# The last layer's gate weights move beside its first products, and its last products go tile by tile to the output

## The reference

```python
x = _rmsnorm(src + sa, norm1_w)              # rows of 256, 512 of them
shared = _swiglu(flat @ W_shared_in) @ W_shared_out
g_probs = jax.nn.softmax(flat @ Wg_gate + group_bias, -1)      # 2 groups
g_idx = jnp.argmax(g_probs, axis=-1)
e_logits = flat @ We_gate + expert_bias                        # 8 experts
e_probs = jax.nn.softmax(jnp.where(in_group, e_logits, -jnp.inf), -1)
p_expert = e_probs * g_prob
topv, topi = jax.lax.top_k(p_expert, TOPK)                     # w: top 2, else 0
h = _swiglu(flat @ W1_shared)                                  # silu(a) * b
for e in range(E):
    routed = routed + h @ W2_experts[e] * w[:, e:e + 1]
out = _rmsnorm(x + (shared + routed), norm2_w)                 # added to the layer's input
```

## Time and profile before

| what | value |
|---|---|
| median of 3 runs | 2666.93 us (2666.87 to 2674.51) |
| the profiled execution's own time | 2669.26 us |
| its span, first to last instruction | 2667.4 us |
| TensorE busy | 2354.3 us, 88% of the span |
| DVE busy | 1460.5 us, 55% |
| ACT busy | 1055.5 us, 40% |
| mean granted TensorE clock | 0.921 of full speed |

### The profile page before, as it was taken

The page is one execution under the profiler, slowest core; times in us unless marked ns, Lnnn a source line. Parts: engine busy times, 40 slices in busy tenths (PEclk is TensorE's granted clock), DMA queues, the critical chain, the costliest instruction groups (busy, mean ns, idle before and its releaser), DMA issues. The chain is left out here.

```text
span 2667.4 us, 38992 instructions
## 1 busy us (share of the span) xinstructions
PE 2354.3 (88%) x15232; PEld 1367.6 (51%) x15232; DVE 1460.5 (55%) x2285; ACT 1055.5 (40%) x1896; POOL 381.9 (14%) x659
## 2 busy tenths in 40 slices
PE   2899999988999998999997687886879999988778
PEld 1344444435699663454453444352238657464547
DVE  4777877623222456888884685226976332323333
ACT  2466666612111233777774372124422233120310
POOL 2454000000000400000001250002630000000000
PEclk8799999998999997999999768987999999888789
DMA  7977553120554699456430001001025240101100
GB/s 197 234 186 166 103 114 57 26 99 2 228 204 175 167 302 236 93 93 133 93 60 35 12 1 61 29 1 65 0 91 178 95 174 0 52 1 51 54 0 8
DMA packets 108359, 258.62 MB, mean 97 GB/s; under 512 B 11824, under 2 KB 83088, under 8 KB 94224
## 3 DMA queue, kind: packets, MB, share of 16 engines
q1 hardware_dynamic: 104144, 213.73, 30.1%
q0 software_dynamic: 2736, 39.37, 4.4%
q10 hardware_dynamic: 1296, 3.03, 0.3%
HBM read 211.26 MB, written 44.83 MB: 96 GB/s over the span
## 5 line engine op out<-in xcount | busy, mean ns | idle before, releaser
L704 DVE TENSOR_REDUCE sta_parts<-sta_psA 128x1 f32<-128x1024 f32 x544 | 626.0, 1188 | 187.4 <-PE sta_psA L621 185.7
L762 ACT ACTIVATE sta_probs<-sta_psS 128x512 f32<-128x512 f32 x1056 | 575.8, 596 | 274.1 <-PE sta_psS L632 272.2
L632 PE MATMUL sta_psS<-L_xattn_qS,L_xattn_kst 99*128 99x256 bf16 x2112 | 356.1, 278 | 11.3 <-ACT sta_probs L762 6.6
L621 PE MATMUL sta_psA<-L_xattn_kst,L_xattn_qS 99*128 99x512 bf16 x1088 | 293.3, 387 | 46.5 <-PEq L59 32.0
L632 PEld LDWEIGHTS sta_psS<-L_xattn_qS,L_xattn_kst 99*128 99x128 bf16 x2112 | 161.6, 98 | 258.8 <-ACT sta_probs L762 183.2
L641 PE MATMUL sta_psO<-sta_probs,L_xattna_V 128*32 128x256 f32 x2560 | 189.5, 385 | 0.0
L621 PEld LDWEIGHTS sta_psA<-L_xattn_kst,L_xattn_qS 99*128 99x128 bf16 x1088 | 104.3, 99 | 131.3 <-DVE sta_parts L704 43.5
L235 ACT ACT_TABLE_LOAD x14 | 18.0, 1283 | 262.1 <-PEq L59 262.1
L1046 ACT ACTIVATE sht_probs<-sht_psS 128x768 f32<-128x768 f32 (+1 forms) x64 | 55.3, 864 | 151.5 <-PE sht_psS L890 100.0
L641 PE MATMUL sta_psO<-sta_probs,L_xattn_V 128*32 128x256 f32 x1536 | 114.8, 390 | 0.0
L481 POOL CAST sta_split<-sta_neg 128x2 bf16<-128x2 f32 x64 | 12.2, 190 | 715.4 <-issue 467.4
(11 more groups left out here) (631 smaller groups left out, 4012.3 us busy)
## 6 DMA issues: line engine op xcount, KB each, us to landing
L_xattn_kst<-L_xattn_keys SPq DMA_DIRECT2D x186, 136.0 KB, 5.0
L_xattn_kst<-L_xattn_keys SPq DMA_DIRECT2D x186, 128.0 KB, 4.7
L_xattn_values<-prj_rows SPq DMA_DIRECT2D x64, 256.0 KB, 3.8
L_xattn_keys<-prj_parts SPq DMA_DIRECT2D x32, 384.0 KB, 4.0
L_xattna_V<-in_ctxV SPq DMA_DIRECT2D x5, 2048.0 KB, 11.7
L_xattna_V<-L_xattn_values SPq DMA_DIRECT2D x5, 2048.0 KB, 10.7
l2f_W<-in_M SPq DMA_DIRECT2D x10, 1024.0 KB, 8.8
L_xattn_keys<-sta_bparts SPq DMA_DIRECT2D x24, 384.0 KB, 7.1
```

What stands on the lines that cost most here:

```text
L621: last = nc.tensor.matmul(psA[:, u % 2, col:col + rhs.shape[1]], lhsT, rhs, start=True, stop=True)
L632: last = nc.tensor.matmul(psS[:, at % 2, j * T:(j + 1) * T], lhsT, rhs, start=True, stop=True)
L704: nc.vector.tensor_reduce(into(parts[:, u // n % 2]), view(psA[:, u % 2, :]), AX.X, ALU.max).then_inc(max_taken, 1)
L762: nc.scalar.activation(probs[:, u % NP, i * 512:(i + 1) * 512], psS[:, at % 2, :], ACT.Exp, scale=scale).then_inc(probs_ready, 1)
```

## The change

- In `rope_and_groups` the four small products with `gates` stand ahead of the eight Silu products. `group_weights` no longer is a stage; it returns two functions, and `gemms` calls them by its new argument `beside`: DVE makes the gate weights after its four copies of `logit`, in the same stage as the Silu products; ACT does the two Exp right after its first Silu.
- The third products, the normalisation, the addition and the store become one stage, `expert_rows`. The products go tile by tile (nine for a tile) round six PSUM banks. After each tile DVE takes its statistics (`measure`), ACT its Sqrt, DVE normalises and adds X (`close`), and SP issues that tile's transfer.
- `gemms` has two more semaphores in every call, `asked` and `answered`.

```diff
--- before.py
+++ after.py
@@ -252,7 +252,8 @@
                     nc.tensor.matmul(psI[:], K["ident16"], K["mask16_q"], start=True, stop=True)
-def gemms(nc, K, jobs, ring=4, loads=(), vector=(), scalar=(), await_loads=None, begin=()):
+def gemms(nc, K, jobs, ring=4, loads=(), vector=(), scalar=(), await_loads=None, begin=(), beside=None):
@@ -262,8 +263,8 @@
     with pool(nc, f"gem{nc.next_id()}") as p:
         banks = p.ps("banks", [P, ring, 512])
         turn = [sum(1 for j in jobs[:n] if j[4] == jobs[n][4]) for n in range(len(jobs))]
-        with stage(nc, "product_ready", "dve_took", "act_took", "dve_step", "act_step", "loaded") as \
-                (block, product_ready, dve_took, act_took, dve_step, act_step, loaded):
+        with stage(nc, "product_ready", "dve_took", "act_took", "dve_step", "act_step", "loaded", "asked", "answered") as \
+                (block, product_ready, dve_took, act_took, dve_step, act_step, loaded, asked, answered):
             took = {"v": dve_took, "s": act_took}
             def view(n):
@@ -302,6 +303,9 @@
                     if job[4] == "v":
                         dve.wait_ge(product_ready, n + 1)
                         job[3](view(n), step).then_inc(dve_took, 1)
+                if beside:
+                    dve.wait_ge(dve_took, sum(job[4] == "v" for job in jobs))
+                    beside[0](dve, step, asked, answered)
             @block.scalar
             def _(act):
@@ -312,6 +316,8 @@
                     if job[4] == "s":
                         act.wait_ge(product_ready, n + 1)
                         job[3](view(n), step).then_inc(act_took, 1)
+                        if beside and turn[n] == 0:
+                            beside[1](act, asked, answered)
 def vcopy(nc, dst):
@@ -2731,85 +2737,151 @@
         hT = p.sb("hT", [P, 2 * HC, NTOK])
         logit = p.sb("logit", [P, NT, 2 + E])
         gate = p.sb("gate", [P, NT, E])
-        gemms(nc, K, [(P, NTOK, [(we[n][:, k, m * P:(m + 1) * P], x1T[:, k, :]) for k in range(KC)],
-                       (lambda ps, step, i=i, m=m: nc.scalar.activation(sil[:, i * HC + m, :], ps, ACT.Silu)), "s")
-                      for i, n in enumerate(("in", "w1")) for m in range(HC)]
-              + project_rows(we["gates"], 2 + E, x1T, lambda t: vcopy(nc, logit[:, t, :]), "v", bias=we["bgates"], ones=K["ones"][0:1, :]))
+        gemms(nc, K, project_rows(we["gates"], 2 + E, x1T, lambda t: vcopy(nc, logit[:, t, :]), "v", bias=we["bgates"], ones=K["ones"][0:1, :])
+              + [(P, NTOK, [(we[n][:, k, m * P:(m + 1) * P], x1T[:, k, :]) for k in range(KC)],
+                  (lambda ps, step, i=i, m=m: nc.scalar.activation(sil[:, i * HC + m, :], ps, ACT.Silu)), "s")
+                 for i, n in enumerate(("in", "w1")) for m in range(HC)], beside=group_weights(nc, p, logit, gate))
         gemms(nc, K, [(P, NTOK, [(we[n][:, k, HID + m * P:HID + (m + 1) * P], x1T[:, k, :]) for k in range(KC)],
                        (lambda ps, step, i=i, m=m: nc.vector.tensor_tensor(hT[:, i * HC + m, :], ps, sil[:, i * HC + m, :], ALU.mult)), "v")
                       for i, n in enumerate(("in", "w1")) for m in range(HC)])
-        group_weights(nc, p, logit, gate)
-        gemms(nc, K, project_rows(we["out"], C, hT, lambda t: vadd(nc, acc[:, t, :], x1[:, t, :]), "v", kc=HC)
-              + [(P, C, [(hT[:, HC + k, t * P:(t + 1) * P], we["w2"][:, e * HC + k, :]) for k in range(HC)],
-                  (lambda ps, step, e=e, t=t: nc.vector.scalar_tensor_tensor(out=acc[:, t, :], in0=ps, scalar=gate[:, t, e:e + 1], in1=acc[:, t, :],
-                                                                            op0=ALU.mult, op1=ALU.add)), "v")
-                 for e in range(E) for t in range(NT)])
-        normalize(nc, K, acc, s1, None, 1e-6, rms=True, w=w["norm2_w"])
-        with stage(nc, "added") as (block, added):
+        expert_rows(nc, K, p, X, x1, acc, s1, hT, gate, we, w["norm2_w"], K["out"])
+def expert_rows(nc, K, p, X, x1, acc, rows, hT, gate, we, weight, out):
+    HC, RING = hT.shape[1] // 2, 6
+    stats = p.sb("end_stats", [P, NT, 6])
+    mv = p.sb("end_mv", [P, NT, 2])
+    var = p.sb("end_var", [P, NT])
+    sd = p.sb("end_sd", [P, NT + 1])
+    one = p.sb("end_one", [P, NT])
+    with pool(nc, "end") as p1:
+        banks = p1.ps("banks", [P, RING, 512])
+        with stage(nc, "product_ready", "taken", "dve_step", "var_ready", "sd_ready", "rows_ready", "stored") as \
+                (block, product_ready, taken, dve_step, var_ready, sd_ready, rows_ready, stored):
+            @block.tensor
+            def _(pe):
+                for n in range(NT * (E + 1)):
+                    t, e = n // (E + 1), n % (E + 1)
+                    if n >= RING:
+                        pe.wait_ge(taken, n - RING + 1)
+                    for k in range(HC):
+                        terms = (hT[:, k, t * P:(t + 1) * P], we["out"][:, k, 0:C]) if e == 0 else \
+                            (hT[:, HC + k, t * P:(t + 1) * P], we["w2"][:, (e - 1) * HC + k, :])
+                        last = nc.tensor.matmul(banks[:, n % RING, 0:C], *terms, start=k == 0, stop=k == HC - 1)
+                    last.then_inc(product_ready, 1)
             @block.vector
             def _(dve):
-                nc.vector.tensor_tensor(X[:], X[:], s1[:], ALU.add).then_inc(added, 1)
-                dve.wait_ge(added, 1)
+                step = Steps(dve, dve_step)
+                V = nc.vector
+                def add_up(t):
+                    for e in range(E + 1):
+                        n = t * (E + 1) + e
+                        dve.wait_ge(product_ready, n + 1)
+                        ps = banks[:, n % RING, 0:C]
+                        if e == 0:
+                            V.tensor_tensor(acc[:, t, :], ps, x1[:, t, :], ALU.add).then_inc(taken, 1)
+                        else:
+                            V.scalar_tensor_tensor(out=acc[:, t, :], in0=ps, scalar=gate[:, t, e - 1:e], in1=acc[:, t, :],
+                                                   op0=ALU.mult, op1=ALU.add).then_inc(taken, 1)
+                        dve.wait_ge(taken, n + 1)
+                def measure(t):
+                    mean, square = mv[:, t, 0:1], one[:, t:t + 1]
+                    step(V.bn_stats(stats[:, t, :], acc[:, t, :]))
+                    step(V.bn_aggr(mv[:, t, :], stats[:, t, :]))
+                    step(V.tensor_tensor(square, mean, mean, ALU.mult))
+                    step(V.tensor_tensor(square, square, mv[:, t, 1:2], ALU.add))
+                    V.tensor_scalar(var[:, t:t + 1], square, 1e-6, None, ALU.add).then_inc(var_ready, 1)
+                def close(t):
+                    dve.wait_ge(sd_ready, t + 1)
+                    step(V.reciprocal(one[:, t:t + 1], sd[:, t:t + 1]))
+                    step(V.tensor_scalar(rows[:, t, :], acc[:, t, :], one[:, t:t + 1], None, ALU.mult))
+                    step(V.tensor_tensor(rows[:, t, :], rows[:, t, :], weight[:, :], ALU.mult))
+                    V.tensor_tensor(rows[:, t, :], X[:, t, :], rows[:, t, :], ALU.add).then_inc(rows_ready, 1)
+                for t in range(NT):
+                    add_up(t)
+                    measure(t)
+                    close(t)
+            @block.scalar
+            def _(act):
+                nc.scalar.activation(sd[:, NT:NT + 1], K["ones"][:, 0:1], ACT.Sqrt)
+                for t in range(NT):
+                    act.wait_ge(var_ready, t + 1)
+                    nc.scalar.activation(sd[:, t:t + 1], var[:, t:t + 1], ACT.Sqrt).then_inc(sd_ready, 1)
+            @block.sync
+            def _(sp):
+                for t in range(NT):
+                    sp.wait_ge(rows_ready, t + 1)
+                    sp.dma_start(out[t // TB, (t % TB) * P:(t % TB + 1) * P, :], rows[:, t, :]).then_inc(stored, 16)
+                sp.wait_ge(stored, 16 * NT)
 def group_weights(nc, p, logit, gate):
     G, EG = 2, E // 2
     names = ("gmax", "gsum", "gp", "emax", "esum", "ep", "prob", "rank", "cmp")
     shapes = ((P, NT), (P, NT), (P, NT, G), (P, NT, G), (P, NT, G), (P, NT, E), (P, NT, E), (P, NT, E), (P, NT, E))
     gmax, gsum, gp, emax, esum, ep, prob, rank, cmp = (p.sb(n, list(s)) for n, s in zip(names, shapes))
-    with stage(nc, "dve_step", "shifted", "exp_ready") as (block, dve_step, shifted, exp_ready):
-        @block.scalar
-        def _(act):
-            act.wait_ge(shifted, 2)
-            nc.scalar.activation(gp[:], gp[:], ACT.Exp).then_inc(exp_ready, 1)
-            nc.scalar.activation(ep[:], ep[:], ACT.Exp).then_inc(exp_ready, 1)
...
+    def by_act(act, asked, answered):
+        act.wait_ge(asked, 2)
+        nc.scalar.activation(gp[:], gp[:], ACT.Exp).then_inc(answered, 1)
+        nc.scalar.activation(ep[:], ep[:], ACT.Exp).then_inc(answered, 1)
...
+    return by_dve, by_act
...
@@ -2859,6 +2931,7 @@
         K["expert_loads"] = [fetches.enter_context(nc.semaphore(f"expert_loads{i}")) for i in range(3)]
```

(47 more changed lines are left out.)

38 lines of the change are left out of this document (removed).

## The result

The changed kernel takes 2660.14 us (median of 10 runs, 2653.4 to 2666.11), the kernel before 2670.36 us beside it (10 runs, 2666.49 to 2675.72): ratio 0.9961, interval 0.9948 to 0.9974, some 10 us less. The forecast was 20.4 us less; 2660.14 lies outside its range.

What follows compares the result with a forecast made beforehand. TensorE, busy 88%, was taken to set the pace of the products, DVE alone that of the gate stage. +0.4 - 11.4 - 5.0 + 2.0 - 6.4 = -20.4 us from 2666.93 gave 2646.5 us, range 2643 to 2651 us.

Steps and rivals of the forecast that it cites:

- The first stage's end: First products of the last layer: the stage now ends with the last Silu instead of a copy, +0.4 us.
- The gate stage: Between second and third products: the separate DVE stage goes and one barrier of 0.31 us stays, -11.4 us.
- The cover: First products: DVE's gate chain would end 1.1 us before the last Silu, so its work counts as nothing.
- The clock: Second and third products: TensorE no longer runs partly at 1.2 GHz there, -5.0 us.
- The dip: First products: small products now at the head lower the clock at about 2547, slowing dense ones, +2.0 to +3.0, taken +2.0 us.
- the two rises: Old profile, third and second products: the clock came back 3.9 us or 6.0 us after dense work began.
- The end: From the last taking of a third product to the program's end: 5.9 us instead of 12.3, -6.4 us.
- Everything else: All 31 gemms calls: POOL clears two more semaphores after each, taken as 0, bound +2.7 us.
- a part lost: Rival, last layer: gate chain, low clock or tile closing takes back 3 to 10 us, 2649.5 to 2656.5 us; chance 0.14.
- a gain without a dip: Rival, first products: small products do not lower the clock, so +2.0 falls away, 2644.5 us; chance 0.22.
- The sign that I named for being wrong: Ahead of the last layer: steps before 2543 us changing in length would show the prediction wrong; no size given.

Runs made afterwards that it cites:

- e2: The changed kernel with the two semaphores made only in the one gemms call that uses them; 2647.88 us, ratio 0.9927 to the kernel before.
- e8: e2 with one dense Silu product ahead of the four small ones; 2649.15 us, ratio 0.9933 to the kernel before.
- e6: The kernel before with a second clear of one semaphore behind each gemms, 31 clears more, no new semaphore; 2670.17 us, ratio 0.9998.
- e1: The kernel before with only the two further, unused semaphores in each gemms call; 2679.21 us, ratio 1.0034.
- e7: The kernel before with two small DVE stores (0.25 us) at the end of the stage ahead of the state-space stage; 2676.45 us, ratio 1.0029.
- e9: The kernel before with one small DVE store (0.12 us) at the end of the stage ahead of the state-space stage; 2678.16 us, ratio 1.0036.
- e11: e2 with one small DVE store (0.12 us) ahead of the state-space stage; 2659.0 us, ratio 0.9959 to the kernel before.
- e5: The kernel before with the two further semaphores in each gemms call, never cleared by POOL; 2674.22 us, ratio 1.0020.

## Why the prediction missed, by its own steps

*The first stage's end, +0.4.* Right: it ends with a Silu of 0.60 us where a copy of 0.17 was.

*The gate stage, -11.4.* Right: TensorE's gap is 1.05 us where it was 12.47. The cover was said to be 1.1 us. e2 shows just that (DVE's last step ends at 2558.96, the last Silu at 2560.06); the changed kernel shows 1.9 us, since its dense products ended later in a longer dip. The Exp start where the table load ends (1.28 us behind 2561.79), and the load starts 0.02 us behind a Silu: the drain of some 1.38 us that the Trainium skill's page "ScalarE: Activation LUTs" (section on what ACT_TABLE_LOAD costs) adds for each switch isn't there, between two tables in use as little as behind an idle ACT. By the page's figure, as an estimate, the gate chain would have ended 1.4 us later here, still 0.5 us ahead of the last Silu.

*The clock, -5.0.* Right: 2.98 us in the second products, 64.32 - 62.40 = 1.9 us in the third.

*The dip, +2.0.* The right mechanism, mis-sized: 2573.94 - 2553.31 = 20.6 us of TensorE's work where 17.29 were, +3.3 us, above the bound of 3.0. I let the clock fall at the end of the small products. It fell 2.5 us behind the first of them, so they ran slow themselves (4.04 us up to the dense ones, where they had taken 3.48), and it held for 6.8 us in all; of the two rises that I had, the longer one was nearer. In e2 it was 1.7 us, in e8 there was none: this term varies with what stands around it.

*The end, -6.4.* Right: 5.8 us from the last taking to the end where it was 12.3.

Sum in the last layer: +0.4 - 11.4 - 4.9 + 3.3 - 6.5 = -19.1, and -19.0 is measured.

*Everything else, "I take 0, bound +2.7".* This is the step that failed: some 9 us stood where it had 0. It priced the two semaphores by the time that POOL takes to clear them (62 clears; the changed kernel has 46 more than e2). That time costs nothing that can be measured (e6). But the semaphores alone slow the kernel before by 9 us (e1), and the changed kernel without them is 9 us faster by the ratios, 12 by the medians (e2): tested in both directions. Of the rivals none spoke of this: that of a part lost (0.14) gives 2649.5 to 2656.5 us, still under the result, by waits or a longer low clock in the last layer, of which only 1.3 us of clock came; a gain without a dip (0.22) is what e8 shows in that stage, not the changed kernel. The sign that I named for being wrong, steps ahead of 2543 us that change in length, is what came.

What the runs show of the mechanism: in the state-space stage the added time goes with two or three more stretches at 1.2 GHz, in nearly the same places in the changed kernel, e1, e7, e9 and e11; a delay of 0.12 us directly ahead of it is enough to bring them, and put into e2 it makes a kernel of the changed kernel's time. The two semaphores make such a delay: 0.29 us at a barrier 28 us ahead of the stage, of which 0.18 us are left against the clock at its start. That stage is 5.3 of some 9 us; the rest lies in small pieces elsewhere that I didn't test singly.

What stays open: why POOL is 0.3 us late at one barrier more when the program has more semaphores or clears. It is so in e1, e5, e6 and the changed kernel, and the place differs; one run (e6) of POOL's instructions alone doesn't say what sets it. Why the clock falls for some starts of the stage and not for others isn't shown either, only that it does. Each kernel has one profile, so the table above is one execution of each. Nor do I know whether the kernel before stands in a lucky place: e6 left it undisturbed, and of the delays tried ahead of the stage all made it slower and none faster.

The best version is e2, 0.9927, with e8 beside it; both beat the kernel before and the changed kernel.

## What to carry to other kernels

An edit to a helper that all stages share is an edit to all stages: make the new semaphores only in the call that needs them, and when a local change brings less than its own part of the trace shows, compare start times and granted clocks of the parts ahead of it before doubting its mechanism. Where TensorE's clock has several low stretches, a difference of 0.3% can come from 0.1 us in the wrong place, so run the kernel before with a tiny neutral delay or two before a result of that size is believed, in either direction. Where TensorE has a few microseconds of small products at the head of a stage, try them behind a dense product: here that took the low stretch away, though its 1.6 us couldn't be measured in the whole.
